# Filling the gap between two graph layers and splitting the last group's finish into four units

## The reference

```
def gnn0(x, inp, adj, w0):
    scores = where(adj > 0, x @ w0 @ inp.T, NEG_PAD)
    return softmax(scores / 0.07, axis=1) @ inp

def gnn1(x, adj, W, a1, a2):
    Wh = x @ W
    e = leaky_relu((Wh @ a1)[:, None] + (Wh @ a2)[None, :], 0.2)
    return elu(softmax(where(adj > 0, e, NEG_INF), axis=1) @ Wh)

x = layernorm(x + gnn0(x, L0_gnn_input, adj, L0_gnn_weight))
return layernorm(x + gnn1(x, adj, L1_gnn_W, L1_gnn_a1, L1_gnn_a2))
```

## Time and profile before

| | before |
|---|---|
| median of 3 runs | 1446.47 us (1445.7 to 1446.51) |
| profiled execution | 1446.21 us |
| its span | 1444.2 us |
| TensorE busy | 1408.1 us (98%) |
| VectorE busy | 1295.0 us (90%) |
| GpSimd busy | 1193.5 us (83%) |
| ScalarE busy | 1107.8 us (77%) |

### The profile page before, as it was taken

The page is one execution under the profiler, slowest core; times in us unless marked ns, Lnnn a source line. Parts: engine busy times, 40 slices in busy tenths (PEclk is TensorE's granted clock), DMA queues, the critical chain, the costliest instruction groups (busy, mean ns, idle before and its releaser), DMA issues.

```text
span 1444.2 us, 28536 instructions
## 1 busy us (share of the span) xinstructions
PE 1408.1 (98%) x9695; PEld 1015.6 (70%) x9695; DVE 1295.0 (90%) x2169; ACT 1107.8 (77%) x2478; POOL 1193.5 (83%) x890
## 2 busy tenths in 40 slices
PE   8899999999999999999999999989999999999996
PEld 4577777777777777777777777765666666666764
DVE  6899999999999899998999999869899999999996
ACT  6788888888888888888888888868757566656564
POOL 7788888888888888888888878848989989898984
PEclk9899999999999999999999999998999999999998
DMA  8999999999999999999999989764434444344420
GB/s 268 285 271 262 264 259 258 274 268 273 274 254 264 257 267 270 271 273 263 259 264 253 277 267 272 194 136 89 106 67 102 88 92 92 86 88 102 88 59 15
DMA packets 427921, 291.41 MB, mean 202 GB/s; under 512 B 356865, under 2 KB 403201, under 8 KB 427777
## 3 DMA queue, kind: packets, MB, share of 16 engines
q1 hardware_dynamic: 427776, 289.59, 73.3%
HBM read 160.56 MB, written 40.89 MB: 139 GB/s over the span
## 4 chain that ended last, share of the span: by engine, by line
PE 91%; POOL 3%; DVE 2%; ACT 2%; issue 1%; DMA 0%; ACTq 0%; POOLq 0%; SPq 0%; DVEq 0%
PE ps L656 17%; PE ps L682 12%; PE ps L738 11%; PE ps L748 10%; PE ps L658 9%; PE ps L693 8%; PE ps L695 8%; PE ps L694 8%; PE ps L719 6%; POOL p_lo L567 2%; PE ps L762 1%; PE ps L626 1%; DVE rows L1066 1%; POOL rstd L577 1%; DVE neg_mask L1031 1%
## 5 line engine op out<-in xcount | busy, mean ns | idle before, releaser
L885 ACT ACTIVATE rows<-rows,exp_bias 128x512 f32<-128x512 f32 x576 | 417.3, 725 | 55.9 <-DVE exp_bias L1041 55.8
L567 POOL TENSOR_TENSOR p_lo<-p,p_hi 128x1024 fp32r<-128x1024 f32 x171 | 404.0, 2408 | 34.8 <-ACT p_hi L933 25.0
L1066 DVE CUSTOM_DVE_ANT_0 rows<-ps,neg_mask 128x1024 f32<-128x1024 f32 x288 | 352.1, 1223 | 80.9 <-PE ps L695 73.5
L475 POOL TENSOR_SCALAR edges<-neg_mask 128x1536 uint8<-128x1536 bf16 x190 | 307.7, 1620 | 97.8 <-DVE neg_mask L1031 85.9
L1160 DVE SCALAR_TENSOR_TENSOR p<-ps,e_col,edgesT 128x1024 f32<-128x1024 f32 x288 | 349.4, 1274 | 10.9 <-PE ps L712 6.8
L656 PE MATMUL ps<-vals,pT_hi 128*128 128x256 f16 x1536 | 295.4, 273 | 1.0 <-ACT att L864 0.8
L871 ACT CAST pT_hi<-ps 128x512 f16<-128x512 f32 x384 | 223.2, 581 | 92.2 <-PE ps L682 92.2
L517 POOL TENSOR_TENSOR inp_sb<-rows,inp_sb 128x512 f16<-128x512 f32 x192 | 281.5, 1487 | 8.2 <-DVE inp_sb L1075 0.7
L933 ACT CAST p_hi<-p 128x1024 fp32r<-128x1024 f32 x196 | 199.6, 1047 | 107.8 <-DVE p L1160 99.3
L658 PE MATMUL ps<-vals,pT_lo 128*128 128x128 f16 x1536 | 274.7, 219 | 0.0
L1082 DVE TENSOR_TENSOR pT_lo<-ps,pT_hi 128x512 f16<-128x512 f32 x384 | 250.8, 683 | 4.9 <-ACT pT_hi L871 4.9
(11 more groups left out here) (126 smaller groups left out, 1948.2 us busy)
## 6 DMA issues: line engine op xcount, KB each, us to landing
adj_sb<-adj SPq DMA_DIRECT2D x192, 768.0 KB, 5.5
edge_rows<-edges SPq DMA_DIRECT2D x192, 192.0 KB, 4.8
xq<-x SPq DMA_DIRECT2D x48, 64.0 KB, 2.9
xr<-x SPq DMA_DIRECT2D x48, 64.0 KB, 5.7
out<-y_w SPq DMA_DIRECT2D x5, 512.0 KB, 3.5
inp_sb<-inp SPq DMA_DIRECT2D x3, 768.0 KB, 8.3
inp_sb<-inp_sb SPq DMA_TRANSPOSE x96, 4.6
edgesT<-edge_rows SPq DMA_TRANSPOSE x48, 5.3
```

The source lines that it names most:

```text
L567: nc.gpsimd.tensor_tensor(p1_lo[:, m % LO_SLOTS, :], p1[:, (NB * g + n) % P_SLOTS, :], p1_hi[:, m % HI_SLOTS, :].bitcast(F32), ALU.subtrac ...
L885: nc.scalar.activation(row_chunk(1 - par, c), row_chunk(1 - par, c), ACT.Exp, bias=exp_bias[:, 1 - par:2 - par], scale=EXP_SCALE, accum_ou ...
L1066: nc.vector.tensor_tensor_reduce(row_pair(par, k), scores_pair(k), neg_mask_row[:, 2 * k * CHUNK:2 * (k + 1) * CHUNK], 1.0, -3.0e38, ALU.a ...
```

## The change

- **Between the layers**: keep_busy issues plain matmuls of the constants averager and ident into bank ACC0, whose result nothing reads: 14 ahead of the transpose of s_top and 3 behind the mean's product (the table IDLE_FILL; its middle entry is 0). mean_of_wh is cut in two, and both parts now stand here: mean_row behind the transpose of s_top, the product behind spread_r. VectorE makes the repeated mean ahead of group 0's first weights.
- **First block plain**: split_of now has block 1 split and block 0 plain, in every group. ScalarE's loop has high_part of block n ahead of the values of block n + 4.
- **Last tile's sums**: tile 47 adds in bank MISC instead of PV (tile_sum), and its chunk 4 waits for xT_lo of tile 47 instead of for the copy of tile 46's sums.
- **Last group's finish**: four units of two tiles. Each unit has a bank of its own for its output tiles and one for its exponentials. The second half of the sums is copied in two pieces of 256 columns, unit three waits for the first and unit four for both. The last unit's two tiles are both normalized by VectorE, without ScalarE's and GpSimd's steps for it.

```
-            return (n * 30) % NB < 30 and n not in DVE_LOWS
+            return n == 1 or n > 1 and (n * 30) % NB < 30 and n not in DVE_LOWS
...
-            return (ACC0 + 2 * par + k // 4, k % 4) if k % 4 < 3 else (R_ROW + k // 4, 0)
+            return ACC0 + (2 * par, 2 * (1 - par), 2 * (1 - par) + 1, 2 * par + 1)[k // 2], k % 2
...
+        def ex_unit(w):
+            q, lo, hi = units[w]
+            return ex_rows if q < NG - 1 else two_rows((EX0, EX0 + 1, R_ROW, R_ROW + 1)[lo // 2])
...
-        units = [(q, 0, GT) for q in range(NG - 1)] + [(NG - 1, 0, GT // 2), (NG - 1, GT // 2, GT)]
+        units = [(q, 0, GT) for q in range(NG - 1)] + [(NG - 1, k, k + 2) for k in range(0, GT, 2)]
...
+        def tile_sum(tile):
+            return ps[:, PV if tile < NB - 1 else MISC, 0:2 * P]
...
                 if bc == MOVED:
-                    after(pe, att_out, t_of)
-                acc = ps[:, PV, 0:2 * P]
+                    if t_of < NB - 1:
+                        after(pe, att_out, t_of)
+                    else:
+                        pe.wait_ge(xT_lo_set, NB)
+                acc = tile_sum(t_of)
...
-                pe.wait_ge(accT_set, q + 1 if lo == 0 else q + 2)
+                pe.wait_ge(accT_set, q + 1 if lo < GT // 2 else q + lo // 2)
...
+            def keep_busy(count):
+                for i in range(count):
+                    nc.tensor.matmul(ps[:, ACC0, 0:P], averager[:], ident[:], start=True, stop=True)
+
             pe.wait_ge(masked, PAIRS * NB)
+            pe.wait_ge(avg_set, 2)
+            keep_busy(IDLE_FILL[0])
             pe.wait_ge(s_part, 1)
             nc.tensor.transpose(ps[:, SPARE, 2 * P:3 * P], s_top[:, 0:1].to_broadcast([P, P]), ident[:]).then_inc(s_spread, 1)
+            mean_row()
+            keep_busy(IDLE_FILL[1])
             pe.wait_ge(r_set, 1)
             spread_r(0)
+            mean_of_wh()
+            keep_busy(IDLE_FILL[2])
...
-                    if n == 8 and g == 0:
-                        mean_of_wh()
...
                     if i == 1 and n == NB - HALVED + 2:
-                        finish_unit(units_of(NG - 1)[0])
-            finish_unit(units_of(NG - 1)[1])
+                        for w in units_of(NG - 1)[:2]:
+                            finish_unit(w)
+            for w in units_of(NG - 1)[2:]:
+                finish_unit(w)
...
-                nc.scalar.copy(accT[:, i * CHUNK:(i + 1) * CHUNK], acc_half((NG - 1) % 2, i)).then_inc(accT_set, 1)
+                    nc.scalar.copy(accT[:, 0:CHUNK], acc_half((NG - 1) % 2, 0)).then_inc(accT_set, 1)
+                else:
+                    for a in (0, 2 * P):
+                        nc.scalar.copy(accT[:, CHUNK + a:CHUNK + a + 2 * P],
+                                       acc_half((NG - 1) % 2, 1)[:, a:a + 2 * P]).then_inc(accT_set, 1)
...
-                    if g == 0 and n + 4 < NB:
-                        make_vals1(n + 4)
                     if 0 < g < NG and n == 4:
                         acc_out(g - 1)
                     if g < NG and by_dve(g, n):
                         copy_rows(g, n)
                     if g < NG and (split_in(g, n) or by_dve(g, n)):
                         high_part(g, n)
+                    if g == 0 and n + 4 < NB:
+                        make_vals1(n + 4)
...
+            dve.wait_ge(mean_turned, 1)
+            nc.vector.tensor_scalar(mean_rep[:], mean_ps.to_broadcast([P, P]), 1.0 / NB, None, ALU.mult).then_inc(mean_repd, 1)
...
-                for k in range(lo + 1, hi, 2):
+                for k in range(lo if w == LAST_UNIT else lo + 1, hi, 1 if w == LAST_UNIT else 2):
```

More of the change, by code:

```diff
@@ L220, in build, with two_rows, h_unit @@
         ex_rows = ps[:, EX0:EX0 + 2, :].rearrange("p b (k d) -> p (b k) d", d=P)
+        def two_rows(bank):
+            return ps[:, bank, 0:2 * P].rearrange("p (k d) -> p k d", d=P)
+        def h_unit(w):
+            q, lo, hi = units[w]
+            return h_rows(q % 2) if q < NG - 1 else two_rows(out_place(q, lo)[0])
+        def ex_unit(w):
+            q, lo, hi = units[w]
+            return ex_rows if q < NG - 1 else two_rows((EX0, EX0 + 1, R_ROW, R_ROW + 1)[lo // 2])
         p1_ps = ps[:, EX0:EX0 + 2, :].rearrange("p b w -> p (b w)")
-        units = [(q, 0, GT) for q in range(NG - 1)] + [(NG - 1, 0, GT // 2), (NG - 1, GT // 2, GT)]
+        units = [(q, 0, GT) for q in range(NG - 1)] + [(NG - 1, k, k + 2) for k in range(0, GT, 2)]
         def units_of(g):
             return [w for w, unit in enumerate(units) if unit[0] == g]
+        LAST_UNIT = len(units) - 1
         def units_until(g):
@@ L952, in elu_parts @@
                 for k in range(lo, hi):
[L953 removed]
+                    op = nc.scalar.activation(h[:, k - lo, :], u_w[:, k, :], ACT.Copy, scale=inv[:, k:k + 1])
                 op.then_inc(h_set, 1)
@@ L960, in elu_parts @@
                 after(act, dve_lo_set, dves_until(q + 1, 0))
-                nc.scalar.activation(ex_rows[:, lo:hi, :], neg_w[:, lo:hi, :], ACT.Exp, scale=-1.0).then_inc(ex_set, 1)
+                if q == NG - 1:
+                    act.wait_ge(p1_set, NB * NG)
+                nc.scalar.activation(ex_unit(w), neg_w[:, lo:hi, :], ACT.Exp, scale=-1.0).then_inc(ex_set, 1)
             def normalize(w):
@@ L996, in _ @@
                         for i, w in enumerate(units_of(g - 1)):
-                            if g == NG:
-                                acc_half_out(i)
+                            if g == NG and i % 2 == 0:
+                                acc_half_out(i // 2)
                             elu_parts(w)
@@ L1274, in _ @@
                                 statistics(w)
-            first_half, second_half = units_of(NG - 1)
-            denominators(first_half)
-            numerators(first_half)
-            sum_up(first_half)
-            denominators(second_half)
-            numerators(second_half)
-            statistics(first_half)
-            sum_up(second_half)
-            statistics(second_half)
+            one, two, three, four = units_of(NG - 1)
+            for w in (one, two):
+                denominators(w)
+                numerators(w)
+            sum_up(one)
+            statistics(one)
+            sum_up(two)
+            for w in (three, four):
+                denominators(w)
+                numerators(w)
+            statistics(two)
+            for w in (three, four):
+                sum_up(w)
+                statistics(w)
             for w in units_of(NG - 1):
```

30 lines of the change are left out of this document (16 added, 14 removed).

## The result

The changed kernel takes **1436.38 us** in the median (1435.43 to 1437.67, 6 runs); the kernel before, run beside it, 1445.3 us (1443.28 to 1446.51, 6 runs). The ratio is 0.994, 95% interval 0.9928 to 0.9953: 8.7 us less, between 6.8 and 10.4. The direction and the mechanisms of the change held.

The account below looks back on a forecast made before the run. TensorE, 98% busy, was taken as the bound, with time to win where it stands or runs slowly and behind its last product. 0.3 + 3.06 + 1.21 + 2.65 + 0.05 = 7.3 us gave 1439.2 us, range 1437.2 to 1440.8.

Parts of the forecast that it names:

- The clock between the layers: Between layers 1 and 2, with fillers in TensorE's idle time: 2.4 GHz expected throughout.
- the first rival: Between the layers the clock falls despite fillers: gain 0.5 in place of 3.06 us, 1441.8 us; chance 0.17.
- Last tile, 0.3: End of layer 1: tile 47's sums in bank MISC bring the last chunk 0.3 us earlier, bounds 0 and 0.81.
- Start of layer 2, 3.06: Block 4 of layer 2 starts 3.06 us earlier, by faster transposes, full-clock products and a start without p_hi.
- The mean, 1.21: Mean's three products and two waits leave layer 2's product stream for the gap between layers: 1.21 us.
- Supply behind it, 0: Layer 2 after its start: GpSimd's low parts and the other engines keep up with earlier products, cost 0.
- The slower rival: Start of groups 1 to 5: TensorE waits for GpSimd's low parts, 2.36 us each, 1451.0 us; chance 0.04.
- The end, 2.65: Tail after the last product: smaller units, VectorE the bound, finish 2.65 us earlier; bounds 0.5 and 3.3.
- The last store, 0.05: Final store of 128 KB, against 256 KB before: taken as 0.05 us gained.
- The rivals' sum: Both the clock falling between layers and small units losing the tail's gain: 1443.6 us; chance 0.04.
- Clock and tail together: Combined case: clock falls between layers (alone 0.17), tail gains only 0.5 us (alone 0.13); together 1443.6 us, chance 0.04.
- the base of the sum: Whole kernel: starting time, the profiled execution's 1446.21 us, with the median of three runs 0.26 above it.

Follow-up runs that it names:

- experiment 1: Changed kernel without its 17 filler matmuls: 1439.13 us, ratio to the kernel before 0.9958.
- experiment 2: Kernel before plus fillers only, 14 ahead of the score sum's transpose and 4 behind the spread of r: 1444.15 us, ratio 0.9993.
- experiment 3: Changed kernel with block 0 of layer 2 split again and ScalarE's order as before: 1439.17 us, ratio to the kernel before 0.9959.
- experiment 4: Changed kernel with the mean's three matmuls and VectorE copy back behind block 8 of layer 2: 1440.11 us, ratio to the kernel before 0.9964.
- experiment 5: Changed kernel with the last group's output in two units of four tiles, second half copied in one piece: 1440.17 us, ratio to the kernel before 0.9965.
- experiment 12: Kernel before plus 20 filler matmuls in layer 1's first tiles (8, 4 and 8): 1443.68 us, ratio to the kernel before 0.9989.

## Why the prediction was right and wrong, step by step

- **The clock between the layers** (the first rival): stayed full from 966 us on, as forecast. Experiments 1 and 2 show that it needs the fillers and more than the fillers.
- **Last tile, 0.3:** measured 0.37 and, undone, 0.36. That other operations set the pace soon after was the right reason to take less than half of the 0.81: in the changed kernel TensorE stands 0.25 us at 956.54 for a pT_lo.
- **Start of layer 2, 3.06:** measured 2.96 at block 4, 2.94 at block 6. Blocks 1 and 2 started 2.22 and 1.61 us behind the block before them, worked out were 2.26 and 1.60. "About 0.9 of this is the transposes; the rest is products at the full clock and the start without p_hi" named the two parts but treated them as a sum; they are conditions for one another (experiments 2, 3).
- **The mean, 1.21:** right as a difference of the two traces, wrong as the price of that edit. "VectorE comes 0.94 earlier" was in the text, beside TensorE's 3.06; the gap between the two is a wait, and with the mean left in the stream it would have taken 1.38 us of the gain (experiment 4).
- **Supply behind it, 0:** TensorE has no wait for p_lo in layer 2, and block 9 to the last product is 434.63 us against 434.77. The slower rival is excluded.
- **The end, 2.65:** measured 2.96. The widths were good: 0.42 on VectorE (taken 0.43), 0.38 to 0.39 on ScalarE (0.38), 0.71 on GpSimd (0.72), and VectorE is the bound. VectorE began its work behind the last product 2.26 us after that product's start, exactly as worked out; the steps from there on were taken 0.3 too long, so that the last y ends 9.98 us behind the start of the last product, by my steps 10.28. The Trainium skill's page "VectorE: DVE Perf Modes", section on the TRN2 errata, asks for at least 512 elements an operation. What it has of a fixed part agrees (256 columns 0.42, 512 0.69), but the conclusion doesn't hold at the end of a chain through four engines, where four units of narrower operations instead of two, with the last two tiles both on VectorE, gave 2.75 us (2.96 less the 0.21 of the two copies).
- **The last store, 0.05: mis-sized.** It is 0.41 by the two traces, 0.48 in experiment 5; landing 1.8 us against 2.1 gives 0.3 of it. "Half the bytes can give nothing or half of that; I take 0.05, near nothing, since the issue and the landing stay" was a choice without a row behind it. The Trainium skill's page "DMA: Bandwidth & Descriptors", section "Anatomy of one DMA", by which the estimate was 0.3, was nearer.
- **The rivals' sum.** Clock and tail together give 0.5 and 0.5 in place of 3.06 and 2.65, that is 1443.9 by the forecast's own terms and not 1443.6. The forecast doesn't rest on it.
- **The step that failed: the base of the sum.** The terms come to 8.03 measured for 7.3 forecast, and by that alone it would have been 1438.4, inside the range. "The profiled execution took 1446.21 us (span 1444.2), so 1438.9; the median of the three runs is 0.26 above it" took everything that the change doesn't touch as fixed. But that execution had the low clock in layer 1, and the three runs lay within 0.8 us of one another beside it. Later runs of the same kernel go down to 1443.16 us, and three of the changed kernel's six are under 1436. The miss of 2.8 us is made up of 0.7 from the terms, 1.2 from the base (1446.47 taken, 1445.3 in the median of the six runs beside the changed kernel) and 0.9 by which the two medians are further apart than the traces' 8.03. Experiment 12 shows that the low clock of layer 1 is behind such a shift: with it gone, the kernel before takes 1443.68 and not 1445.64. Why the changed kernel has the full clock there more often, which the 0.9 would ask for, stays open. The range needed a term for the clock of stretches outside the change, about 2.4 us to the lower side; the profile of before showed 0.50 at 48 to 52 us, and I did not look there.

What stays open: what decides which clock an execution gets in layer 1, since the same idle piece before 34 us (2.13 or 2.14 us) is followed by either clock; why the kernel before seldom comes near its lowest times (of 21 runs beside experiment 12 two are under 1443.2, the median is 1445.64) where the changed one does in half of its runs, though their layer 1 is the same. Experiment 12 offers a reason that these runs don't prove: in the kernel before an earlier layer 1 can be paid back by a longer low clock between the layers, which the fillers there exclude. The mean's move by itself was not tried.

## What to carry to other kernels

Before a sum is made against a profiled execution, read the granted clock over the whole span, not only where the change is: here a stretch at 1.2 GHz behind an idle piece of 2.1 us ran at 2.4 GHz in other executions, and the forecast's range had to hold the 2.4 us that hung on it. (The idle piece of 3.84 or 3.85 us between the layers was followed by the low clock in all four profiles that have it.) When an edit lets one engine start earlier, ask how far the others move up with it; the difference turns into a wait at the next point where they meet, and moving that meeting point is then worth more than the time it takes in the old trace. At the end of a kernel, where nothing else is left to overlap, try halving the units and the stores even though each operation gets less efficient; here that won 3.4 us (experiment 5).

## What the runs showed of the hardware that I had not expected

- The same idle piece has two outcomes. Behind the first piece of 2.13 to 2.18 us, before 34 us, the clock fell to half in eight profiles and stayed full in four. What follows then differs: the eight, slower at first, have only 0.6 to 0.8 us of idle time before 39 us but 2.61 before 48, and fall there again; the four have 2.23 to 2.26 us before 39 and fall behind it (0.50 in 40 to 43 us), at no visible cost. The eight have the att copy of tile 0 up to 2.6 us later.
- The low clock has no fixed length. Between the layers it lasted 10.2 us in the kernel before, 13.6 us with an earlier layer 1, and about 3.4 us in experiment 2, where TensorE went straight into dense products; each time it came back only a few microseconds after dense products had begun (978.14 to 982.2 in the kernel before, 975.58 to 981.7 in experiment 12, 976.75 to 980.6 in experiment 2).
- Matmuls that compute nothing made the kernel faster: 17 of them are worth 1.90 us (experiment 1), 20 others made the kernel before 2.0 us faster in the median (experiment 12).
